# One attention and mixture-of-experts kernel: the work ahead of the first loop in a new order, on other engines and banks

## The chip, the cores and the metric

The kernel runs on one core of one Trainium2 chip. A core has five engines that run side by side, each through its own list of instructions: TensorE (PE; its weight loads are listed apart as PEld), VectorE (DVE), ScalarE (ACT), GpSimd (POOL) and SyncE (SP), which here only issues DMA transfers. They wait for each other through semaphores. Sixteen DMA engines move data between memory and the on-chip buffer; TensorE writes its results into eight banks of a second buffer, PSUM, which VectorE and ScalarE read. The metric is the time of one execution on the device, in microseconds (us).

## What is computed

The input is x, 16 sequences of 512 tokens of 128 numbers. First comes attention with a gated linear recurrence, then a mixture of eight experts with the two best for each token; both are wrapped in layer norms and residuals.

```python
x = x + layernorm(attention(layernorm(x)))
x = x + layernorm(experts(layernorm(x)))

# attention: 16 query heads over 4 key/value heads of 64
q = relu(split(h @ Wq, 16)); k = relu(split(h @ Wk, 4)); v = split(h @ Wv, 4)
g = log_sigmoid(split(h @ Wg1 @ Wg2 + bg2, 4)) / 16
S_t = exp(g_t)[:, None] * S_{t-1} + k_t (outer) v_t ; o_t = (q_t * scale) @ S_t
o = g_norm_weight * o * rsqrt(mean(o**2) + eps)
out = o.reshape(b, t, 1024) @ Wo
```

## The kernel before

The program is in float32. It goes over the 16 sequences one after the other, one turn of a loop for each; a sequence has four tiles of 128 tokens (`NT`) and eight chunks of 64 (`NC`). Within a turn, `chunks(i)` computes the outputs of sequence i chunk by chunk, and between these the next sequence's norm, gates, keys, values, queries and states are prepared: `norm_stats`, `norm_apply`, `norm_transposes`, `gate_logits`, `gates`, `gate_logs`, `gate_sum`, `gate_scan`, `gate_relative`, `decays`, `project_keys`, `project_values`, `key_transposes`, `project_queries_and_states`. The key transposes end in `kJ`, the values in `vJ`, and the state updates (L550) read both; L560 (`scores`) is the first matmul of `chunks`. After the sixteen turns the tokens are sorted to experts, the expert tiles run in a second loop, and a last stage sums and normalises.

Each engine's order is written out by hand. The preparation of sequence 0 has nothing to lie beside, so the same functions run once ahead of the loop, and that stretch is what the change touches. There:

- SP first gives twelve credits to semaphores, then issues the load of the first tokens (`xa`, L380), the eleven loads of the list `WEIGHTS` (L382, with `cst` last, a table of constants of 692 KB that also holds the 0/1 row `in_chunk` for the scan), and the three large expert weights (L384). All count into one semaphore, `weights_in`.
- DVE waits for all of `WEIGHTS`, then makes eight constants (L1262 to L1270, among them the zeroing of `zeros` and `kT`), and only then the statistics of the first tokens (L1026, L1030).
- ACT waits for the weights, for `vJ` to be zeroed and for all eight constants before its table load (L927) and the root of the variance (L767, L769).
- POOL zeroes `vJ` (L1480), applies the norm (L1389), adds the two parts of the gates (`gate_sum`, L1398) and makes them relative to the middle of each chunk (`gate_relative`, L1408). DVE does the scan between these two (L1034).
- PE puts both gate logits (L494, for the head pairs p = 0 and 1) into the one bank `pJ[0]`; the second waits until ACT has read the first twice (L784, L787). Keys, values, key transposes, then all queries mixed with the states follow.

In the loop the functions keep POOL for the norm and for the two gate steps.

## Time and profile before

| | us |
|---|---|
| median of 3 runs | 1332.94 |
| lowest, highest | 1332.85, 1337.09 |
| the profiled execution | 1333.82 |
| its span in the trace | 1332.0 |

PE is busy for 1240.2 us of the span (93%), DVE for 789.2, ACT for 674.4 and POOL for 552.0. The page's chain that ended last lies to 65% on PE. Of 40 equal slices PE is at nine tenths or more in nearly all; the first slice has three tenths, and a few late ones (at the change to the experts and in the last stage) have less.

Times in a trace count from the start of the span. A row gives a start, a duration and what the engine did; `x4` behind it means that four instructions were merged. `[4.09 <-POOL xn L1389]` says that the engine had been idle for 4.09 us and that the named work released it. A float32 matmul leaves two records.

### The profile page before, as it was taken

Reading aid. Unit: us, or ns where it says so; the run is one execution under the profiler, and the core shown is the slowest. Engines: PE = TensorE matmul, PEld = TensorE weight load, DVE = VectorE, ACT = ScalarE, POOL = GpSimd, SP = SyncE. Lnnn points to the kernel's source line nnn. Section 1 sums busy time; section 2 is a strip of 40 time slices with the busy share of each in tenths; the row PEclk is TensorE's granted clock in tenths of the full one; section 3 lists DMA queues with packets and bytes.
Section 4 is the critical chain, followed back from the end, with each engine's and each line's share of the span. In section 5 each row is a group of like instructions: output and inputs, shape, how many; then the busy total and the mean of one; then the engine's idle time right before and its main releaser. Section 6 shows DMA issues by size and latency. Waiting matters only on the chain.

```text
span 1332.0 us, 27589 instructions
## 1 busy us (share of the span) xinstructions
PE 1240.2 (93%) x8008; PEld 1037.8 (78%) x8008; DVE 789.2 (59%) x2374; ACT 674.4 (51%) x1717; POOL 552.0 (41%) x674
## 2 busy tenths in 40 slices
PE   3999999999999999999999999939999999999975
PEld 1778788787787787887877877828899999988952
DVE  2667767767777777677677777643333333333327
ACT  2466565475465665654754656423444444443426
POOL 2223534535436446355354364142333333333326
PEclk9999999999999999999999999969999999999998
DMA  7000100101101001001011010033311111111164
GB/s 274 9 17 9 41 14 26 32 13 34 32 8 40 21 18 40 12 28 32 12 36 32 8 32 16 21 141 106 104 48 48 51 49 48 49 46 44 48 229 178
DMA packets 60282, 67.99 MB, mean 51 GB/s; under 512 B 7488, under 2 KB 50144, under 8 KB 59872
## 3 DMA queue, kind: packets, MB, share of 16 engines
q1 hardware_dynamic: 50656, 46.03, 10.8%
q0 software_dynamic: 8448, 17.45, 4.0%
q10 hardware_dynamic: 1152, 4.19, 1.1%
q8 instruction: 12, 0.20, 0.1%
q14 instruction: 14, 0.11, 0.0%
HBM read 38.50 MB, written 29.15 MB: 51 GB/s over the span
## 4 chain that ended last, share of the span: by engine, by line
PE 65%; DVE 13%; issue 8%; DMA 4%; ACT 4%; POOL 3%; DVEq 1%; SPq 0%; POOLq 0%; ACTq 0%
PE pO L723 8%; PE pA L560 8%; PE pO L576 8%; PE pO L578 6%; PE pW L605 4%; PE pA L714 4%; PE pA L715 4%; PE pJ L714 4%; PE pJ L715 4%; PE pT L588 3%; PE pJ L494 2%; PE pJ L605 2%; DVE S_raw L1076 2%; PE pA L542 2%; DMA expert_out<-y,tail 2%
## 5 line engine op out<-in xcount | busy, mean ns | idle before, releaser
L1524 POOL DMA_INDIRECT expert_out<-y,tail x136 | 130.1, 957 | 264.1 <-ACT y L985 236.9
L576 PE MATMUL pO<-vJ,aT 128*128 128x128 f32 x1024 | 194.1, 279 | 0.0
L578 PE MATMUL pO<-S_mid,qT 128*128 128x128 f32 x896 | 173.2, 275 | 0.0
L840 ACT ACTIVATE sq<-pO 128x512 f32<-128x512 f32 x128 | 75.8, 592 | 184.8 <-PE pO L576 142.2
L576 PEld LDWEIGHTS pO<-vJ,aT 128*128 128x128 f32 x1024 | 153.8, 192 | 14.6 <-issue 13.2
L1099 DVE TENSOR_REDUCE ss<-sq 128x8 f32<-128x512 f32 x128 | 86.5, 676 | 100.6 <-ACT sq L840 100.6
L1458 POOL DMA_INDIRECT expert_rows<-x1n,rowi x120 | 117.1, 976 | 64.9 <-issue 39.5
L578 PEld LDWEIGHTS pO<-S_mid,qT 128*128 128x128 f32 x896 | 136.1, 192 | 0.0
L560 PE MATMUL pA<-qT,kT 128*128 128x256 f32 x512 | 133.3, 383 | 2.5 <-DVE qT L1060 2.5
L723 PE MATMUL pO<-wdown_sb,vJ 128*128 128x128 f32 x1088 | 132.7, 275 | 0.0
L723 PEld LDWEIGHTS pO<-wdown_sb,vJ 128*128 128x128 f32 x1088 | 126.8, 192 | 0.0
L1333 DVE TENSOR_TENSOR vJ<-pA,kJ 128x256 f32<-128x256 f32 x136 | 57.6, 425 | 109.1 <-ACT kJ L976 109.1
L550 PEld LDWEIGHTS pO<-vJ,kJ 128*128 128x128 f32 x448 | 65.2, 190 | 61.8 <-issue 23.1
L605 PE MATMUL pW<-wo_sb,oT 128*128 128x128 f32 x768 | 96.9, 280 | 6.4 <-ACT oT L853 6.4
L1106 DVE TENSOR_TENSOR arena<-pO,rs 128x512 f32<-128x512 f32 x128 | 88.6, 692 | 20.9 <-ACT rs L848 18.9
L605 PEld LDWEIGHTS pW<-wo_sb,oT 128*128 128x128 f32 x768 | 92.4, 195 | 10.2 <-issue 8.3
L560 PEld LDWEIGHTS pA<-qT,kT 128*128 128x128 f32 x512 | 87.4, 191 | 15.5 <-DVE qT L1060 8.9
L853 ACT ACTIVATE oT<-pT,gn_sb 128x512 f32<-128x512 f32 x128 | 86.5, 676 | 22.8 <-PE pT L588 20.7
L985 ACT ACTIVATE y<-pO,tail 128x128 f32<-128x128 f32 x136 | 42.4, 363 | 108.5 <-PE pO L723 88.1
L1333 DVE TENSOR_TENSOR vJ<-pJ,kJ 128x256 f32<-128x256 f32 x136 | 57.6, 425 | 59.0 <-ACT kJ L976 59.0
L1092 DVE TENSOR_TENSOR aT<-pA,cst 128x512 f32<-128x512 f32 x128 | 87.7, 685 | 7.2 <-PE pA L560 7.2
L1425 POOL TENSOR_TENSOR S_mid<-S_raw,step 128x256 f32<-128x256 f32 x112 | 68.4, 617 | 51.6 <-DVE S_raw L1076 34.5
(225 smaller groups left out, 2604.0 us busy)
## 6 DMA issues: line engine op xcount, KB each, us to landing
xt<-expert_rows SPq DMA_DIRECT2D x69, 130.0 KB, 2.2
xa<-x SPq DMA_DIRECT2D x16, 256.0 KB, 2.8
xr<-x SPq DMA_DIRECT2D x16, 256.0 KB, 2.8
after_attention<-x SPq DMA_DIRECT2D x16, 256.0 KB, 2.4
arena<-after_attention ACTq DMA_DIRECT2D x8, 512.0 KB, 3.6
expert_rows<-zeros SPq DMA_DIRECT2D x8, 390.0 KB, 3.1
expert_out<-y,tail POOLq DMA_INDIRECT x136, 2.2
wgate_sb<-wgate SPq DMA_DIRECT2D x1, 2048.0 KB, 9.3
```

The costliest lines, as they stand in the source:

```text
L560: last = mm(pA[c % 2][:, p, :], kT[:, p, c, :], qT[:, p, c, :, :].rearrange("p r c -> p (r c)"), start=True, stop=True)
L576: last = mm(o, aT[:, c % 2, p, h * P:(h + 1) * P], vJ[:, c, p, :], start=True, stop=(c == 0))
L578: last = mm(o, qT[:, p, c, 2 * h:2 * h + 2, :].rearrange("p r c -> p (r c)"), S_mid[:, c, p, :], start=False, stop=True)
L605: last = mm(merge_bank[t], oT[:, t % 2, b, :, :].rearrange("p a c -> p (a c)"), wo_sb[:, b, :], start=(b == 0), stop=(b == PAIRS * R - 1))
L714: mm(bank[f][:, 0:ROWS], wgate_sb[:, e, f * P:(f + 1) * P], xtT[:], start=True, stop=True)
L715: mm(bank[f][:, ROWS:2 * ROWS], wup_sb[:, e, f * P:(f + 1) * P], xtT[:], start=True, stop=True).then_inc(up_psum, 1)
L723: last = mm(ybank[k], hT[:, f, k * P:(k + 1) * P], wdown_sb[:, e, f, :], start=(f == 0), stop=(f == FB - 1))
L1092: v.tensor_tensor(aT[:, c % 2, :, :].rearrange("p a (r c) -> p (a r) c", c=C), pA[c % 2][:].rearrange("p a (r c) -> p (a r) c", c=C), wide ...
L1106: v.tensor_tensor(on[:, c % 2, :, :].rearrange("p k (h d) -> p (k h) d", d=D), pO[c % 2][:].rearrange("p k (h d) -> p (k h) d", d=D), wide ...
L1333: v.tensor_tensor(hT[:, f, :], bank[f][:, ROWS:2 * ROWS], sil[:, f, :], ALU.mult)\
L1458: g.indirect_dma_start(out=xs_dram, in_=x1n[:, k, t, :], in_offset=None, out_offset=bass.IndirectOffsetOnAxis(ap=rowi[:, k, t:t + 1], axis ...
L1524: g.indirect_dma_start(out=ys_dram, in_=y[:, k, :], in_offset=None, out_offset=bass.IndirectOffsetOnAxis(ap=tail[:, k, 1:2].bitcast(U32), ...
```

## The change

The edit leaves the loop, the experts and the last stage as they are, and rewrites the start:

- The small weights (`bg2`, `gnorm`, the router's `rw` and `rb`) become columns of `cst`; the row of 1024 scan constants leaves it, so that it shrinks from 1384 to 379 columns. `wg1` and `wg2` travel as one tile. `in_chunk` is made on POOL.
- ACT issues `cst` and `wg` on its own queue, then loads its table, then waits. SP issues `xa`, `wk`, `wv`, `wq`, `wo`, then gives the twelve credits, then issues the large weights. There are four semaphores (`first_in`, `kv_in`, `q_in`, `rest_in`) in the place of one.
- `kT` and `zeros` are zeroed on POOL. DVE does the statistics first and makes its constants later.
- For sequence 0 the norm, `gate_sum` and `gate_relative` are done by DVE. The gate logits go to `pO[0]` and `pO[1]`.
- ACT copies the first half of the values between the two pairs' decays.
- PE projects the first query ahead of the key transposes, and has four groups of matmuls on a blank bfloat16 tile (20, 4, 6 and 24), whose results nobody reads.

```diff
+            def keep_busy(count, bank):
+                for n in range(count):
+                    mm(bank[:, 0:256], blank[:, 0:P], blank[:], start=True, stop=True)
...
+            for dst, src in FIRST_W:
+                act.dma_start(dst[:], src).then_inc(first_in, 16)
             act.preload_act_table_set(LOG_EXP)
+            act.wait_ge(first_in, 16 * len(FIRST_W))
             norm_rstd(0)
             norm_T(0)
...
-            for p in range(PAIRS):
-                decays(0, p)
+            act.wait_ge(vJ_zero, 1)
+            decays(0, 0)
+            values(0, range(0, 1))
+            decays(0, 1)
             steps_of(0)
-            values(0)
+            values(0, range(1, 2))
             keys(0)
...
             for p in range(PAIRS):
+                dve.wait_ge(lz_ready, p + 1)
+                dve.wait_ge(relz_ready, p + 1)
+                v.tensor_tensor(relz[:, p, :], relz[:, p, :], absz[:, p, :], ALU.add).then_inc(gate_ready, 1)
                 gate_scan(0, p)
+                dve.wait_ge(run_ready, p + 1)
+                r3 = run[:, p, :].rearrange("p (n c) -> p n c", c=C)
+                v.tensor_tensor(rel[:, p, :].rearrange("p (n c) -> p n c", c=C), r3,
+                                wide(r3[:, :, mid:mid + 1], P, NC, C), ALU.subtract).then_inc(rel_ready, 1)
             gate_steps(0)
...
+            g.memset(blank[:], 0.0).then_inc(blank_made, 1)
+            g.memset(in_chunk[:], 1.0).then_inc(scan_made, 1)
+            pool.wait_ge(scan_made, 1)
+            settle(pool)
+            g.memset(in_chunk[:].rearrange("p (n c) -> p n c", c=C)[:, :, 0:1], 0.0).then_inc(scan_made, 1)
+            g.memset(kT[:], 0.0).then_inc(kT_zero, 1)
             g.memset(vJ[:], 0.0).then_inc(vJ_zero, 1)
-            norm_apply(0)
-            for p in range(PAIRS):
-                gate_sum(0, p)
-            for p in range(PAIRS):
-                gate_relative(0, p)
+            g.memset(zeros[:], 0.0).then_inc(zeros_made, 1)
             mids(0)
```

On PE, from its first matmul to the key transposes, stood before (`pJ0` to `pO1` are PSUM banks, `xnT` the normed tokens transposed):

```order
L485 MATMUL pT<-wg2_sb,wg1_sb 128x256 [waits const_made,weights_in]
L481 MATMUL pW<-cst,xn 128x128 [waits xn_ready]
L481 MATMUL pW<-cst,xn 128x128 x3
L494 MATMUL pJ0<-xnT,w12_sb 128x512 [waits xnT_ready,w12_ready]
L494 MATMUL pJ0<-xnT,w12_sb 128x512 [waits relz_ready]
L506 MATMUL pJ0<-xnT,wk_sb 128x512 [waits relz_ready]
L506 MATMUL pJ1<-xnT,wk_sb 128x512
L513 MATMUL pA0<-wv_sb,xnT 128x256 x2
L513 MATMUL pA1<-wv_sb,xnT 128x256 x2
L524 MATMUL pO0<-cst,kT 128x128 [waits k_ready]
```

and stands now, in the same stretch (L680 is the blank matmul):

```order
L680 MATMUL pJ1<-blank 128x256 [waits blank_made]
L680 MATMUL pJ1<-blank 128x256 x19
L504 MATMUL pT<-wg_sb 128x256 [waits first_in]
L680 MATMUL pJ1<-blank 128x256 x4
L500 MATMUL pW<-cst,xn 128x128 [waits xn_ready]
L500 MATMUL pW<-cst,xn 128x128 x3
L680 MATMUL pJ1<-blank 128x256 x6
L513 MATMUL pO0<-xnT,w12_sb 128x512 [waits xnT_ready,w12_ready]
L513 MATMUL pO1<-xnT,w12_sb 128x512
L526 MATMUL pJ0<-xnT,wk_sb 128x512 [waits kv_in]
```

The two waits on `relz_ready` are gone, and thirty blank matmuls stand ahead of the logits. Behind the value projections come the 24 others and one query.

On DVE, from the zeroing of `kT` to the step logs, stood before:

```order
L1267 MEMSET kT 128x2048
L1268 TENSOR_SCALAR nbg2_sb<-bg2_sb 128x2
L1270 CAST zeros<-cst 128x6 [waits const_made]
L1026 BN_STATS st<-xa 128x6 [waits xa_in]
L1026 BN_STATS st<-xa 128x6 x3
L1030 BN_AGGR mv<-st 128x2 [waits xn_stat]
L1030 BN_AGGR mv<-st 128x2 x3
L1273 COPY w12_sb<-pT 128x256 [waits w12_psum]
L1034 SCALAR_TENSOR_TENSOR arena<-cst,arena 128x512 [waits gate_ready] x2
L1042 TENSOR_TENSOR step_log<-arena 128x2x7 [waits rel_ready]
```

and now stands, from the last of its constants to the step logs (L1319 is the sum, L1072 the scan, L1323 the relative step):

```order
L1313 CAST zeros<-cst 128x6 [waits zeros_made]
L1319 TENSOR_TENSOR arena<-arena 128x512 [waits relz_ready,lz_ready,scan_made]
L1072 SCALAR_TENSOR_TENSOR arena<-in_chunk,arena 128x512 [waits gate_ready]
L1323 TENSOR_TENSOR arena<-arena 128x512 [waits run_ready]
L1319 TENSOR_TENSOR arena<-arena 128x512 [waits relz_ready,lz_ready]
L1072 SCALAR_TENSOR_TENSOR arena<-in_chunk,arena 128x512 [waits gate_ready]
L1323 TENSOR_TENSOR arena<-arena 128x512 [waits run_ready]
L1080 TENSOR_TENSOR step_log<-arena 128x2x7 [waits rel_ready]
```

The sum, the scan and the relative step of pair 0 now all stand ahead of the sum of pair 1 on one engine, where two scans stood between four instructions of POOL.

## Rows read from the trace of the kernel before

**Rows 1.** Busy us of each engine by stretch; PEclk, DMA share and GB/s end the row.

```profile
0.00:20.00 20.00, 1.19 (x2) 0.50 (x2) 4.70 (x17) 1.78 (x3) 4.52 (x9) 1.00 0.87 324
29.00:33.00 4.00, 3.61 (x5) 1.54 (x6) 1.81 (x2) 1.48 (x3) 2.21 (x2) 1.00 0.00 0
50.00:80.00 30.00, 29.67 (x221) 26.95 (x221) 20.34 (x41) 19.01 (x46) 9.41 (x11) 1.00 0.04 10
```

**Rows 2.** Timeline of all engines, 0 to 52 us: start, us, engine, work.

```profile
0.73 1.80 POOL L1480 MEMSET vJ<- 128x2048 f32 x1 [0.29 <-POOLq L1604]
1.45 0.44 SPq L380 DMA_DIRECT2D xa<-x  x1
...
11.59 0.23 DVE L1262 CAST tri<-cst 128x128 bf16<-128x128 f32 x1 [11.59 <-DMA cst<-consts]
...
15.14 0.86 DVE L1026 BATCH_NORM_STATS2 st<-xa 128x6 f32<-128x128 f32 x4
...
16.15 0.38 DVE L1030 BATCH_NORM_AGGREGATE mv<-st 128x2 f32<-128x6 f32 x4
...
16.96 0.20 ACT L769 ACTIVATE rstd<-lnv 128x4 f32<-128x4 f32 x1
17.47 3.14 POOL L1389 TENSOR_SCALAR xn<-xa,mv,rstd 128x128 f32<-128x128 f32 x4 [14.94 <-ACT rstd L769]
...
20.67 1.12 PE L481 MATMUL pW<-cst,xn 128*128 128x128 f32 x4 [4.09 <-POOL xn L1389]
...
22.56 2.04 PE L494 MATMUL pJ<-xnT,w_sb 128*128 128x512 f32 x2 [0.78 <-ACT xnT L773]
24.64 0.69 ACT L784 ACTIVATE arena<-pJ,bg_sb 128x512 f32<-128x512 f32 x1 [2.23 <-PE pJ L494]
...
28.07 0.69 ACT L784 ACTIVATE arena<-pJ,bg_sb 128x512 f32<-128x512 f32 x1 [0.98 <-PE pJ L494]
...
29.39 3.78 PE L506 MATMUL pJ<-xnT,wk_sb 128*128 128x512 f32 x4 [1.35 <-ACT arena L787]
29.88 0.63 ACT L800 ACTIVATE arena<-arena 128x512 f32<-128x512 f32 x1
...
32.08 2.06 DVE L1034 TENSOR_TENSOR_SCAN arena<-cst,arena 128x512 f32<-128x512 f32 x1 [2.19 <-POOL arena L1398]
...
35.41 0.18 DVE L1042 TENSOR_TENSOR step_log<-arena 128x14 f32<-128x14 f32 x1 [1.27 <-POOL arena L1408]
35.51 2.84 DVE L1051 SCALAR_TENSOR_TENSOR kT<-pJ,arena 64x512 f32<-64x512 f32 x4
...
36.57 3.17 ACT L827 ACTIVATE vJ<-pA 64x256 f32<-64x256 f32 x8
...
39.22 1.88 PE L542 MATMUL pA<-xnT,wq_sb 128*128 128x512 f32 x4
...
39.77 1.08 ACT L835 ACTIVATE kJ<-pO 128x512 f32<-128x512 f32 x2
...
41.67 0.71 PE L550 MATMUL pO<-vJ,kJ 128*128 128x128 f32 x4 [0.57 <-ACT kJ L835]
...
50.05 2.14 PE L560 MATMUL pA<-qT,kT 128*128 128x256 f32 x8
```

**Rows 3.** DMA issues, 0 to 75 us: KB, then us from issue to landing.

```profile
rw_sb<-rw SPq DMA_DIRECT2D x1, 4.0 KB, 3.2
```

**Rows 4.** DMA issues in the first 1.6 us.

```profile
xa<-x SPq DMA_DIRECT2D x1, 256.0 KB, 2.9
```

**Rows 5.** Timeline of PE within the loop: both records of a gate logit.

```profile
60.58 1.02 PE L494 MATMUL pJ<-xnT,w_sb 128*128 128x512 f32 x2
```

**Rows 6.** DVE lines over the span, shortest, median and longest instruction in ns.

```profile
L1190 DVE TENSOR_SCALAR arena<-x,mv,rstd x4: 335/344/365, 869.5 to 880.8; 128x128 f32<-128x128 f32 x4
...
L1034 DVE TENSOR_TENSOR_SCAN arena<-cst,arena x32: 1214/1215/2060, 28.7 to 809.8; 128x512 f32<-128x512 f32 x32
...
L1375 DVE TENSOR_TENSOR S_mid<-S_mid,arena x2: 679/951/1223, 1327.0 to 1328.1; 128x512 f32<-128x512 f32 x2
```

More of the change, by code:

```diff
@@ L57, with build @@
 ACT_TILES = 6
-C_END = C_PAD + PAD_ROWS
-def build(nc, x, wq, wk, wv, wo, wg1, wg2, bg2, gnorm, rw, rb, wgate, wup, wdown, consts, out):
+C_BG = C_PAD + PAD_ROWS
+C_GN = C_BG + PAIRS
+C_RW = C_GN + 1
+C_RB = C_RW + E
+C_END = C_RB + E
+def build(nc, x, wq, wk, wv, wo, wg, wgate, wup, wdown, consts, out):
     S, L, _ = x.shape
@@ L105, in build @@
         iota8 = cst[:, C_IOTA:C_IOTA + E]
+        bg2_sb = cst[:, C_BG:C_BG + PAIRS]
+        gn_sb = cst[:, C_GN:C_GN + 1]
+        rw_sb = cst[:, C_RW:C_RW + E]
+        rb_sb = cst[:, C_RB:C_RB + E]
         ones_row = cst[:, C_ONES:C_ONES + E]
-        in_chunk = cst[:, C_SCAN:C_SCAN + 1024]
+        in_chunk = sb("in_chunk", [P, L])
         tri = sb("tri", [P, P], BF16)
@@ L246, in build @@
         vJ_zero = sem("vJ_zero")
-        weights_in = sem("weights_in")
+        first_in = sem("first_in")
+        kv_in = sem("kv_in")
+        q_in = sem("q_in")
+        rest_in = sem("rest_in")
+        nbg2_made = sem("nbg2_made")
+        scan_made = sem("scan_made")
+        blank_made = sem("blank_made")
+        kT_zero = sem("kT_zero")
+        zeros_made = sem("zeros_made")
         const_made = sem("const_made")
@@ L817, in steps_of, with values @@
                   scale=-1.0 / GATE_NORMALIZER).then_inc(step_ready, 1)
-            def values(j):
-                for g in range(NT // 2):
+            def values(j, groups=range(NT // 2)):
+                for g in groups:
                     act.wait_ge(v_psum, j * 2 + g + 1)
@@ L1259, in places @@
                 v.tensor_copy(rows_at[:, :, part], rowf[:, :, part]).then_inc(rowi_ready, 1)
-            dve.wait_ge(weights_in, 16 * len(WEIGHTS))
+            norm_stats(0)
+            dve.wait_ge(first_in, 16 * len(FIRST_W))
+            v.tensor_scalar(nbg2_sb[:], bg2_sb, -1.0, None, ALU.mult).then_inc(nbg2_made, 1)
+            dve.wait_ge(xn_rstd, 1)
+            for t in range(NT):
+                v.tensor_scalar(xn[:, t, :], xa[:, t, :], mv[:, 0, t, 0:1], rstd[:, 0, t:t + 1],
+                                ALU.subtract, ALU.mult).then_inc(xn_ready, 1)
+            dve.wait_ge(w12_psum, 1)
+            v.tensor_copy(w12_sb[:].rearrange("k p j -> k (p j)"), pT[:, 0:PAIRS * P]).then_inc(w12_ready, 1)
             v.tensor_copy(tri[:], cst[:, C_TRI:C_TRI + P]).then_inc(const_made, 1)
```

96 lines of the change are left out of this document (51 added, 45 removed).

## The prediction

> **What bounds the kernel now.** I read the busy time by stretch first. In the first 20 us PE works for 1.19 us, while in the loop (50 to 80 us) it works for 29.67 of 30 [rows 1]. So the loop is bound by PE and the change leaves it alone; what can be won lies ahead of 50.05, where the first `scores` start [rows 2]. From there every engine's work hangs on that matmul in the same order as before, so a start that comes earlier by some us should bring the end forward by as much.
>
> The timeline of that stretch is a relay with one runner at a time [rows 2]. DVE is released by `cst` at 11.59. It makes constants until 15.14, does the statistics until 16.53 (16.15 + 0.38), and ACT's root ends at 17.16. POOL applies the norm until PE transposes at 20.67. PE starts the first logit at 22.56 and ACT reads it at 24.64. ACT's second pair starts at 28.07 after 0.98 us of waiting for PE and ends at 30.51. Sum, scan and relative step of pair 1 lead to the step logs at 35.41; `kT` is done at 38.35; the copies into `kJ` start at 39.77 behind ACT's value copies and let PE go on at 41.67. From 41.67 to 50.05 PE alternates states and queries, the same before and after the edit.
>
> **The sum, leg by leg.** Each leg is the time before less the time after.
>
> 1. *Loads and statistics.* Three things leave the path: twelve credits ahead of `xa`, ten loads and the large `cst`, and DVE's constants. `xa` was issued at 1.45 [rows 2] behind the credits; POOL's own first work starts at 0.73 [rows 2], so I take 0.8. It landed 2.9 us after its issue [rows 4], which gives 3.7. The statistics took 1.39 (15.14 to 16.53) and end at 5.1 instead of 16.53: **11.4**. If SP cannot issue before 1.45, this is 0.65 less. ACT also needs `cst` and `wg`, two issues of some 0.44 each [rows 2] from 0.75 on; a small load landed in 3.2 [rows 3], so `wg` is in at 4.4, ahead of the statistics. The table load lies in this wait too. The load of the next tokens is issued some 13 us earlier, still behind the large weights. By 29 no DMA runs any more [rows 1], and the next tokens are not read before the chunks begin, at 31 by this sum.
> 2. *The root* keeps its 0.63 and ends at 5.75.
> 3. *The norm.* On POOL it took 3.51 (17.16 to 20.67) [rows 2]. Four like instructions on DVE took 335 to 365 ns each [rows 6]: 1.4, with the hand-over 1.45. Gain **2.05**; xn is ready at 7.2.
> 4. *Transposes.* Both records of a gate logit took 2.04 at 22.56 [rows 2] and take 1.02 in the loop [rows 5]. PE therefore runs at half its later pace at the start, 1.2 GHz against 2.4. The four transposes (1.12) would take 0.56: gain **0.55** if the blank matmuls have brought PE to full pace by 7.2. The first logit then starts at 8.5.
> 5. *First logit.* 2.08 (22.56 to 24.64) becomes 1.08: gain **1.0**. ACT begins at 9.6.
> 6. *Second bank.* The second logit no longer waits for ACT, so the 0.98 of idle time [rows 2] goes. Both pairs take 4.9 instead of 5.87 (24.64 to 30.51): **1.0**. ACT ends at 14.5, with pair 0 done at 12.05.
> 7. *Sum, scan, relative.* DVE has six instructions in a row. A scan takes 1.215; a 128x512 sum of two on-chip tiles took 0.679 undisturbed [rows 6]. That is 2 x (0.68 + 1.215 + 0.68) = 5.15, with six hand-overs of some 0.05 it is 5.45, so 12.1 + 5.45 = 17.55. From ACT's end this is 3.05 where it was 4.9 (30.51 to 35.41): **1.85**. Pair 1's sum is queued behind pair 0's relative step for 0.3 us; this is counted. Bound above: the disturbed prices 1.223 and 2.06 [rows 6] would make the six 9.0, 3.9 us later. I take the undisturbed ones since POOL, once its memsets are over, has nothing to do until the states.
> 8. *Keys.* Step logs to the end of `kT` keep 2.94 (35.41 to 38.35) and end at 20.5.
> 9. *Values and `kJ`.* Eight value copies took 3.2 (36.57 to 39.77) [rows 2] and held the `kJ` copies back. Now four of them fit between pair 0's decays (over at 16.0) and pair 1's at 17.6. Pair 1's two decays and the step take some 1.15 (35.41 to 36.57), the other four values 1.6: ACT is free at 20.35, while the first group of key transposes ends at some 20.9. With 1.9 for the copies (39.77 to 41.67), PE goes on at 22.8, 2.3 behind `kT` instead of 3.3: **0.95**.
>
> Sum: 11.4 + 2.05 + 0.55 + 1.0 + 1.0 + 1.85 + 0.95 = **18.8 us**.
>
> What is costed at nothing: the 24 blank matmuls behind the values. 256 columns at 2.4 GHz are 0.107 us, so 2.6 in all. PE starts the logits at 8.5; two logits, two keys (0.86 each, half of the 1.88 of L542 less its overlap [rows 2]) and the values end near 13.6, the blanks at 16.2, and the first query must wait for values at 17.6 anyway. The cover is 1.4 us. The query itself (0.9) ends at 18.5; pair 0's transposes wait for `kT` at 19.1. POOL's memsets: 2048 columns take 1.80 [rows 2], so blank, `in_chunk`, `kT`, `vJ` and `zeros` together (some 5,400 columns) are done at about 5.8. `vJ` is wanted at 14.8, `kT` at 17.6. SP's credits now stand behind five issues; the loop needs them at 31. DVE's constants (about 1 us) fall behind `w12` at 7.6 and are over before 12.1.
>
> **Two rules weighed.** The column PEclk shows 1.00 from 29 to 33 us [rows 1], where four records of 512 columns took 3.78 against 1.88 for a like four at 39.22 [rows 2]. I go by the durations and count the column as having no record yet. The Trainium skill, "TensorE: Matmul & The Clock Gate", Part 1, warns that the clock gate's trace events have been seen to be unreliable; by the column alone, legs 4 and 5 would be nothing, and the sum 17.25.
>
> The second scan took 2.06 while POOL's L1408 ran beside it, the median of 32 is 1.215 [rows 2, 6]. The Trainium skill, "GPSIMD Engine Reference", section 8, says that GpSimd shares its interfaces to the on-chip buffer with VectorE and contends with instructions that read two tiles there. It speaks against giving POOL 5 us of memsets, if these reach into leg 3; the norm at the same factor of 1.7 would cost 1.0 more and the sum would be 17.8. No row shows a memset beside DVE.
>
> **Rivals.**
>
> *A. The blank matmuls do not lift PE in time, or stand in its way.* Twenty at 1.2 GHz are 4.3 us (0.213 each), so they end at 5.2; then the small product and four more end at about 7.2, just as xn arrives. For it: this leaves no slack, and a blank one could cost more than its columns; a float32 record of 512 columns took 0.94 at half pace (3.78 / 4), which would bound one of 256 at 0.47, and make twenty 9.4. PE came to full pace somewhere between 29.39 and 39.22, that is in less than 9.8 us of nearly steady work. Against it: the blanks begin at 0.95 and PE then has 7 us of steady work before the logits. If the clock rises only around 10, legs 4 and 5 fall out (1.55), six blanks reach 0.5 past the copy, and the twenty delay the start by some more: a gain of 15 to 17, **1317**. If it does not rise at all before the states, logits, keys, values, 24 blanks and the query take 4.1 + 3.8 + 3.8 + 5.1 + 1.9 from 9.6, PE goes on near 31, and the gain is 10.6: **1322**.
>
> *B. The first loads land later.* `cst` and `wg` go on a second queue over the same DMA engines, beside `xa`, keys, values and queries. Each us past 5.1 costs one. At 6.5: a gain of 17.4, **1315.5**. At worst they come behind the large weights, at about 24: nothing is left, **1333**, no change.
>
> *C. Slower.* The early blank work leaves PE at half pace into the loop. There each us of PE's work then costs a second one, as it is busy 99% [rows 1]; it decides at 19 us of such work (38 us of time). The whole of 52 us at half pace would give away 26: **1340**. Against it: with the same loop behind it PE was at full pace from 39.22 on, and nothing in the edit takes work away there.
>
> **How the numbers follow.** The profiled execution took 1333.82, 0.88 above the median of 1332.94. Its own time less 18.8 is 1315.0; from the median it is **1314.1**, my number. Chances: the forecast within 1.5 us 0.62; up to 2.5 us better (loads in 2.4, cheaper norm) 0.06; A in part 0.18, A in full 0.03; B by a us or two 0.07, B in full 0.02; C 0.02. Legs 1, 3 and 7 carry bounds of 0.65, 1.0 and 3.9. The range 1311.5 to 1319 holds the forecast, the better case, A in part and B by little, and leaves out about 1 in 10. Faster by over 0.3% (about what a measurement of this kernel tells from no change) 0.96, within it 0.02, slower 0.02.
>
> **What would show it.** Statistics ending at 5.1 (leg 1); xn to PE in 1.5 (3); both records of the first logit in 1.02 (4, 5); no idle ACT between the pairs (6); step logs at 17.5 (7); L570, the states, at 22.8 (9); the first L580 at 31.2; and a loop of unchanged length. I am wrong if the blanks end after xn is ready, if ACT waits for `first_in` past 5.1, or if the time from the first scores to the end is not 1282 us as it is now (1332.0 - 50.05).

## The result, and the profile after

| | before | after |
|---|---|---|
| median, us (4 runs each, on one chip) | 1333.66 | 1319.48 |
| lowest, highest | 1332.85, 1337.09 | 1318.53, 1321.94 |
| the profiled execution | 1333.82 | 1320.18 |
| its span | 1332.0 | 1318.4 |
| first `scores` | 50.05 | 32.96 |
| from there to the end of the span | 1281.95 | 1285.44 |

The ratio is 0.9892, with a 95% interval of 0.9869 to 0.9915. The change makes the kernel 1.1% faster, on the side that was forecast, but 5.4 us short of 1314.1 and a little past the upper end of 1319.0. The last two rows say where the shortfall lies. The start gained 17.1 us and not 18.8. Then 3.5 us were lost behind it, in code that the change doesn't touch.

The timeline of the new start (start, us, engine, work) answers to [rows 2]:

```profile
0.73 0.44 SPq L393 DMA_DIRECT2D xa<-x  x1
0.74 0.45 ACTq L959 DMA_DIRECT2D cst<-consts  x1
...
1.09 4.24 PE L680 MATMUL pJ<-blank 128*128 128x256 bf16 x20 [1.09 <-POOL blank L1531]
...
4.50 0.87 DVE L1064 BATCH_NORM_STATS2 st<-xa 128x6 f32<-128x128 f32 x4 [4.50 <-DMA xa<-x]
...
6.57 1.12 DVE L1304 TENSOR_SCALAR xn<-xa,mv,rstd 128x128 f32<-128x128 f32 x4 [0.62 <-ACT rstd L803]
...
7.74 0.66 PE L500 MATMUL pW<-cst,xn 128*128 128x128 f32 x4 [1.24 <-DVE xn L1304]
...
9.34 3.11 PE L513 MATMUL pO<-xnT,w_sb 128*128 128x512 f32 x4
...
11.35 0.69 ACT L818 ACTIVATE arena<-pO,cst 128x512 f32<-128x512 f32 x1 [2.33 <-PE pO L513]
...
13.71 0.67 ACT L818 ACTIVATE arena<-pO,cst 128x512 f32<-128x512 f32 x1
...
19.19 0.18 DVE L1080 TENSOR_TENSOR step_log<-arena 128x14 f32<-128x14 f32 x1
...
22.68 1.09 ACT L869 ACTIVATE kJ<-pO 128x512 f32<-128x512 f32 x2 [0.50 <-PE pO L544]
...
24.58 0.71 PE L570 MATMUL pO<-vJ,kJ 128*128 128x128 f32 x4 [0.54 <-ACT kJ L869]
...
32.96 2.14 PE L580 MATMUL pA<-qT,kT 128*128 128x256 f32 x8
```

Of each leg it tells the following.

| leg | forecast | measured |
|---|---|---|
| 1, statistics end | 5.1 | 5.90 |
| 3, norm to PE | 1.45 | 1.21 (6.53 to 7.74) |
| 4 and 5, transposes to ACT's first read | 2.4 | 3.61 (7.74 to 11.35) |
| 6, ACT over both pairs | 4.9 | 4.78, and no idle time at 13.71 |
| 7, ACT's end to step logs | 3.05 | 3.06 (16.13 to 19.19) |
| 8 and 9, step logs to states | 5.25 | 5.39 (19.19 to 24.58) |
| first `scores` | 31.2 | 32.96 |

So two legs missed, 1 by 0.8 us and 4 with 5 by 1.2. The others agree to 0.25. In a second profile of the same kernel (after_again, below) the first `scores` come at 33.19.

Busy us of each engine by stretch (PE, PEld, DVE, ACT, POOL), with PEclk, DMA share and GB/s at the end of a row, answer to [rows 1] and show the second miss:

```profile
6.50:7.70 1.20, 0.00 (x0) 0.00 (x0) 1.14 (x5) 0.03 (x1) 0.00 (x0) 1.00 1.22 475
7.70:8.20 0.50, 0.47 (x4) 0.47 (x5) 0.50 (x3) 0.00 (x0) 0.00 (x0) 1.00 1.12 451
8.20:9.30 1.10, 1.10 (x8) 0.83 (x7) 0.25 (x4) 0.60 (x1) 0.00 (x0) 0.59 0.90 369
9.30:10.00 0.70, 0.70 (x3) 0.38 (x2) 0.00 (x0) 0.00 (x0) 0.00 (x0) 0.50 1.00 421
...
11.90:13.00 1.10, 1.10 (x4) 0.53 (x3) 0.00 (x0) 1.10 (x3) 0.00 (x0) 1.00 0.85 358
```

The blanks had done their work: the transposes took 0.66, not 1.12. But PE stood idle from 6.50 to 7.74, since four blanks do not reach to xn. The granted clock fell from 2.4 to 1.2 GHz near 8.4, though PE was at work again, and rose near 11.8. The first logit lies in the slow part.

The loss behind the start is the harder one. I took the shift between the two profiles (time before less time after, at the same instruction): 17.1 at the first `scores`, 17.3 in turns 4 to 16, and 17.2 at the first transposes of an expert tile (897.00 against 879.77). So the loop, and the sorting behind it, kept the gain. At the last tile it is 14.5 (1278.19 against 1263.72), at the end 13.6. Counted from 0, most of the 69 tiles take 5.46 us in both; the first, tiles 2, 4, 6 and 8 and tile 58 are longer in both. In after, tiles 10, 35 and 59 take 6.92, 6.68 and 7.16. In before these three are normal (5.46, 5.46, 5.53) and tile 52 takes 6.87. Three sound tiles turned long and one long tile turned sound. They are long for two different reasons.

Row transposes of tiles 35 and 36 on PE, after:

```profile
1078.32 0.38 PE L732 MATMUL pT<-cst,xt 128*128 128x128 f32 x2
...
1085.00 0.44 PE L732 MATMUL pT<-cst,xt 128*128 128x128 f32 x2 [1.06 <-DMA xt<-expert_rows]
```

and before:

```profile
1094.12 0.38 PE L698 MATMUL pT<-cst,xt 128*128 128x128 f32 x2
...
1099.58 0.38 PE L698 MATMUL pT<-cst,xt 128*128 128x128 f32 x2
```

The waits of after between 1078 and 1085.5 (us in total, times, longest) lead back from there:

```profile
POOL expert_out L1577 <- ACT y L1023: 4.9, 1, 4.9
ACT y L1023 <- DVE tail L1389: 3.1, 1, 3.1
DVE tail L1389 <- POOLq L1582: 2.7, 1, 2.7
...
PE pT L732 <- DMA xt<-expert_rows: 1.1, 1, 1.1
```

PE waits for the rows `xt`, whose load waited for VectorE, which waited for POOL's queue, which waits at L1582 for the scatter of output rows to land. The DMA queues over the two scatters of this tile (after, 1076.5 to 1080; packets, MB, share) show a guest:

```profile
q8 instruction: 1, 0.02, 2.2%
...
expert_out<-y,tail POOLq DMA_INDIRECT x2, 3.1
```

The 3.1 behind `x2` is the median of the two. Taken alone, the first scatter (1076.61) landed in 2.2 and the second (1077.87), with the packet at 1079.57 beside it, in 4.0. The same tile before (1092.3 to 1096) has no such packet, and its scatters land in 2.2:

```profile
q0 software_dynamic: 64, 0.13, 11.0%
...
expert_out<-y,tail POOLq DMA_INDIRECT x2, 2.2
```

The page's list of queues has, for the whole execution of after (packets, MB, share):

```profile
q8 instruction: 12, 0.20, 0.1%
```

So there are twelve such packets of 16 KB, and their name says that they carry an engine's own instructions. Which engine's, the runs below tell. At tile 10 of after, the scatter in flight beside such a packet took 4.2, and at tile 52 of before 3.8.

The last of the twelve, at 1273.47, meets the very last scatter of after, and the load of the last stage waits for that one. It landed in 6.2 (1272 to 1278); in before the last scatter has no packet beside it and landed in 4.8 (1286.5 to 1292):

```profile
expert_out<-y,tail POOLq DMA_INDIRECT x1, 6.2
```

```profile
expert_out<-y,tail POOLq DMA_INDIRECT x1, 4.8
```

Tile 59 is another matter. No packet stands there. In every profile of this case, before's too, PE waits about 2 us for the rows `xt` at the end of tile 58. PE in after:

```profile
1212.87 0.44 PE L732 MATMUL pT<-cst,xt 128*128 128x128 f32 x2 [2.02 <-DMA xt<-expert_rows]
1213.15 3.49 PE L757 MATMUL pO<-wdown_sb,vJ 128*128 128x128 f32 x16
```

```profile
1214.00:1216.50 2.50, 2.50 (x14) 2.50 (x13) 0.34 (x2) 0.00 (x0) 0.00 (x0) 0.50 0.08 26
```

and in one_queue, a run below whose tile 59 is sound:

```profile
1209.81 0.44 PE L734 MATMUL pT<-cst,xt 128*128 128x128 f32 x2 [2.11 <-DMA xt<-expert_rows]
1210.09 1.96 PE L759 MATMUL pO<-wdown_sb,vJ 128*128 128x128 f32 x16
```

Behind the pause the granted clock fell to 1.2 GHz for some 3 us in after (0.50 in the stretch from 1214.0 to 1216.5), and the sixteen records took 3.49 and not 1.96. This is the loss of legs 4 and 5 once more. It fell so in the ten profiles whose tile 59 is long, and stayed at 1.00 in before, before_longer, aligned and one_queue, with pauses of 1.95 to 2.13 us in all fourteen. Why the same pause lets it fall in some and not in others isn't shown, nor whether it goes by the kernel or by the execution: only after has a second profile, and there it fell too.

### The profile page after: what moved, and what is told of

It is laid out like the page before. It is cut to its first block, busy times and chain, and to the rows that moved or that the text cites. A ratio compares the mean times of both kernels' runs of the same rounds, so it can differ in the third digit from the quotient of the medians.

```text
span 1318.4 us, 27696 instructions
## 1 busy us (share of the span) xinstructions
PE 1243.6 (94%) x8062; PEld 1043.3 (79%) x8062; DVE 789.3 (60%) x2380; ACT 675.0 (51%) x1717; POOL 547.5 (42%) x671
## 4 chain that ended last, share of the span: by engine, by line
PE 66%; DVE 13%; issue 8%; DMA 5%; ACT 4%; POOL 3%; DVEq 1%; POOLq 0%; SPq 0%; ACTq 0%
PE pO L757 8%; PE pA L580 8%; PE pO L596 8%; PE pO L598 6%; PE pW L625 4%; PE pA L748 4%; PE pA L749 4%; PE pJ L748 4%; PE pJ L749 3%; PE pT L608 3%; DMA expert_out<-y,tail 2%; DVE kT L1089 2%; DVE S_raw L1114 2%; PE pJ L625 2%; PE pA L562 2%
## 5 line engine op out<-in xcount | busy, mean ns | idle before, releaser
L887 ACT ACTIVATE oT<-pT,cst 128x512 f32<-128x512 f32 x128 | 86.6, 677 | 22.6 <-PE pT L608 20.8
```

## The experiments

All are edits of after, unless said. "Tiles" is the time from the first to the last row transposes, "long" lists tiles of the four (10, 35, 52, 59) that took over 6.3 us in that kernel's profile. Medians are of four or more runs, and the ratio is against before on the same chip. The kernels were taken on several chips, on which before's own median was 1332.94 (the row here; also for after_again, no_blanks, gap_filled and pool_gates), 1333.53 (late_blanks, aligned, one_queue and one_bank), 1333.66 (after) and 1334.00 (the other four), so over all rows it is the ratios that compare.

| kernel | median | ratio, 95% | first `scores` | tiles | long |
|---|---|---|---|---|---|
| before | 1332.94 | | 50.05 | 381.19 | 52 |
| after | 1319.48 | 0.9892 (0.9869, 0.9915) | 32.96 | 383.95 | 10, 35, 59 |
| after_again | 1319.62 | 0.9889 (0.9873, 0.9905) | 33.19 | 383.28 | 10, 35, 59 |
| no_blanks | 1317.48 | 0.9877 (0.9862, 0.9892) | 33.64 | 381.62 | 52, 59 |
| gap_filled | 1319.09 | 0.9888 (0.9873, 0.9903) | 32.33 | 384.34 | 10, 35, 59 |
| pool_gates | 1325.20 | 0.9934 (0.9920, 0.9947) | 38.43 | 384.36 | 10, 35, 59 |
| late_blanks | 1321.85 | 0.9910 (0.9894, 0.9927) | 33.44 | 383.43 | 10, 35, 59 |
| aligned | 1318.00 | 0.9884 (0.9868, 0.9901) | 31.98 | 380.27 | 52 |
| one_queue | 1317.00 | 0.9878 (0.9862, 0.9895) | 30.92 | 381.36 | 10, 35 |
| one_bank | 1319.64 | 0.9890 (0.9874, 0.9907) | 35.43 | 384.19 | 10, 35, 59 |
| one_queue_aligned | 1316.15 | 0.9866 (0.9851, 0.9882) | 31.39 | 381.63 | 52, 59 |
| before_longer | 1336.76 | 1.0020 (1.0011, 1.0029) | 50.19 | 382.18 | 10, 35 |
| old_query_values | 1320.66 | 0.9898 (0.9882, 0.9913) | 33.09 | 384.21 | 10, 35, 59 |
| one_queue_no_blanks | 1318.52 | 0.9881 (0.9866, 0.9896) | 32.41 | 382.46 | 52, 59 |

**Is the loss a matter of chance?** The changed kernel, unchanged, once more:

> The changed kernel once more, unchanged. In its first profile the first scores start at 32.96 us, 17.1 us earlier than before (50.05), but the end comes only 13.6 us earlier; 3.5 us were lost between the first scores and the end, nearly all in the expert tiles, at tiles whose scatter of output rows finished late (before: one such tile among tiles 10 to 57, at 1187 us; after: two, at 940 and 1078 us, and one more at 1213). Theory 'chance': these late scatters fall where they like in any execution, so this profile has the first scores at 33.0 again (within 0.2) and another number of long tiles, the stretch behind the first scores is 1282 to 1287 us, and over five rounds the gain over the kernel before is near 17 us (15 to 18). Theory 'systematic': the new start brings the later stages into a worse position; the same tiles are long again and the gain stays at 13 to 14.5 us.

The same three tiles are long. The theory that a scatter meets something at random falls; what hits tiles 10 and 35 belongs to the program. The clock at the start does vary: here PE's pause ahead of the transposes was 1.56 us, and the clock had fallen before they began (1.11, not 0.66).

**What are the blanks worth?** All four groups taken out:

```diff
-            keep_busy(20, pJ[1])
...
-            keep_busy(4, pJ[1])
...
-            keep_busy(6, pJ[1])
...
-            keep_busy(24, pW)
```

> The changed kernel without its 54 blank matmuls. In the changed kernel PE's granted clock is full from about 5.2 us, falls to half at about 8.4 (after PE had idled from 6.50 to 7.74) and rises at 11.9, so the first logit (9.34) ran at half pace although the blanks were there. Theory 'the blanks miss': without them the transposes take 1.1 instead of 0.7 and the logit starts at about 9.6, ScalarE's first read begins at 11.7 to 11.9 (11.35 with them), the step logs at 19.5 to 19.8 (19.19), the first scores at 33.2 to 33.8 (32.96): less than 1 us slower. Rival 'the blanks carry the start': keys, values and states run at half pace too and the first scores come at 35 or later, 2 us or more slower.

The logit is then slow from end to end (timeline of no_blanks):

```profile
7.69 1.11 PE L500 MATMUL pW<-cst,xn 128*128 128x128 f32 x4 [1.50 <-DVE xn L1300]
...
9.59 3.75 PE L513 MATMUL pO<-xnT,w_sb 128*128 128x512 f32 x4 [0.78 <-ACT xnT L803]
```

and the first `scores` come 0.45 to 0.7 later than in after and its repeat. Yet the median is 2.1 lower than that of after_again. The intervals of the two ratios overlap, so this is likely and not proven; in the profiles the tiles take 1.7 less, as 10 and 35 are sound again and 52 is long, as in before. If so, the blanks cost more in the experts than they bring at the start, and not by what they do there: they had ended at 18.5. The one thing of them that lasts is that PE's list of instructions is longer, by 54 weight loads and 54 matmuls.

**Does the idle 1.24 us let the clock fall?** The four blanks become fifteen:

```diff
-            keep_busy(4, pJ[1])
+            keep_busy(15, pJ[1])
             norm_transposes(0)
```

> The changed kernel with 15 blank matmuls in the place of 4 ahead of the transposes, which at 0.107 us each reach over the 1.24 us in which PE idled (6.50 to 7.74). Theory 'the idle time dropped the clock': the granted clock stays at full from about 5.2 on, six blanks take 0.65, the first logit starts at 9.1 and takes 1.02, ScalarE's first read begins at 10.2 instead of 11.35, the step logs at 18.1 (19.19) and the first scores at 31.8 (32.96): 1.0 to 1.3 us faster than the changed kernel. Rival 'it falls anyway' (transposes or blanks on zeros don't hold it): the granted clock drops near 8.4 again, the first read begins at 11.3 to 11.6 and nothing is gained, or up to 0.5 us is lost as the blanks stand before the transposes.

```profile
6.50 1.81 PE L680 MATMUL pJ<-blank 128*128 128x256 bf16 x15
...
9.53 1.95 PE L513 MATMUL pO<-xnT,w_sb 128*128 128x512 f32 x4
10.72 0.69 ACT L818 ACTIVATE arena<-pO,cst 128x512 f32<-128x512 f32 x1 [1.34 <-PE pO L513]
```

The logits take 1.95 and not 3.11, and from the transposes to ACT's read it is 2.57 in place of 3.61: 1.0 of the missing 1.2. The granted clock is 1.00 throughout. Some 0.3 of it goes again, as the fifteen run past xn (ready near 7.9, transposed at 8.15), and `xa` landed 0.14 later, so the first `scores` come 0.6 to 0.9 earlier and not the 1.0 to 1.3 expected. The median moved by only 0.5, within the spread, and the tiles stayed as long; in this kernel tile 63 takes 6.87 as well, and there too a packet of queue 8 (between 1234 and 1236) stands beside a scatter, which takes 4.2. With 22 instructions more than after, the packet that met after's last scatter at 1273.47 comes here, and the last scatter lands in 5.3.

**Norm and gate steps back on POOL** (legs 3 and 7):

```diff
-            for t in range(NT):
-                v.tensor_scalar(xn[:, t, :], xa[:, t, :], mv[:, 0, t, 0:1], rstd[:, 0, t:t + 1],
-                                ALU.subtract, ALU.mult).then_inc(xn_ready, 1)
...
+            norm_apply(0)
+            for p in range(PAIRS):
+                gate_sum(0, p)
+            for p in range(PAIRS):
+                gate_relative(0, p)
             mids(0)
```

> The changed kernel with the norm, the sums and the relative steps of sequence 0 back on GpSimd; all else stays. Theory of the forecast: the norm costs 3.5 instead of 1.4 us up to the transposes, and from the end of ScalarE's gates to the step logs it takes 4.9 again instead of 3.1, with the second scan at 2.06 beside GpSimd: 3.5 to 4.2 us slower than the changed kernel, first scores at 36.5 to 37.2. Rival: PE idles longer, the clock stays at half longer, and another 0.5 to 1 us comes on top. If the gates on VectorE were worth nothing, the first scores would stay at 33.

```profile
20.67 2.06 DVE L1072 TENSOR_TENSOR_SCAN arena<-in_chunk,arena 128x512 f32<-128x512 f32 x1 [1.09 <-POOL arena L1438]
...
24.00 0.18 DVE L1080 TENSOR_TENSOR step_log<-arena 128x14 f32<-128x14 f32 x1 [1.27 <-POOL arena L1448]
```

The transposes begin at 10.05, 2.3 later than in after, and the step logs 4.8 later. The scan beside POOL's L1448 takes 2.06 again, as in [rows 2], where after has 1.23. The first `scores` are 5.5 later and the median 5.6 higher. This is more than the 3.5 to 4.2 of the theory: 0.6 more goes at the transposes and the first logit, which stay at half pace throughout, as the rival said, and 0.7 between the step logs and `kJ`. This is the largest single part after the loads.

**Is it the length of PE's code?** No blanks at the start, but 54 of them in the pause ahead of the expert tiles, where PE waits anyway. The start is then that of no_blanks and the code behind as long as after's:

```diff
             pe.wait_ge(tail_in, 16 * len(BIG))
+            pe.wait_ge(an_ready, S * NT)
+            keep_busy(54, pW)
             pe.wait_ge(counts_ready, 1)
```

> No blank matmuls at the start, but 54 of them in the 11 us in which PE idles between the last ranks and the first expert tile (868.5 to 879.8 in the changed kernel). The kernels with 54 or 65 blanks at the start have their long tiles at 10 and 35 in every profile, the one without any has one at 52, as the kernel before; each of these tiles has a 16 KB instruction packet beside its scatter of output rows. Theory 'code length': what counts is how much of PE's code lies ahead of the tile loop, so the long tiles are at 10 and 35 again although the start has no blanks; first tile about 1.3 us shorter (5.5 instead of 6.2 to 7.7) as PE's clock is up when it begins; first scores at 33.6 as without blanks. Rival 'early work': the blanks at the start disturb by what they do there (clock or timing); then the long tile stays at 52.

Tiles 10 and 35 are long again (6.51 and 6.73), as in after, and 52 is sound. The last scatter lands in 6.2, where it took 5.4 in no_blanks. The median is 4.4 above no_blanks, and the intervals of the ratios don't overlap. In the profiles 0.7 of it lies ahead of the first tile, 1.8 in the tiles and 1.3 behind them. That the late blanks would shorten the first tile did not come true: it took 6.58, and 6.21 without them.

In the next kernel the blanks at the start are 20, 11, 4 and 24, and 69 follow late, 128 in all. That makes 256 instructions more than without blanks. The Trainium skill, "Trainium Architecture — The Big Picture", "The software stack", gives an instruction 64 bytes, so by estimate a 16 KB packet holds 256 of them. The runs show the 16 KB and, here, the return of the pattern with 256 instructions more.

```diff
-            keep_busy(4, pJ[1])
+            keep_busy(11, pJ[1])
             norm_transposes(0)
-            keep_busy(6, pJ[1])
+            keep_busy(4, pJ[1])
...
+            pe.wait_ge(an_ready, S * NT)
+            keep_busy(69, pW)
             pe.wait_ge(counts_ready, 1)
```

> The changed kernel with 11 blanks instead of 4 ahead of the transposes and 4 instead of 6 behind them (59 in all), and 69 more in PE's idle stretch ahead of the expert tiles: 128 blanks are 256 instructions or one 16 KB packet of code more than none. Theory 'code length': the packets come at the same tiles as without blanks, so the long tile is at 52 and none at 10 and 35; the clock is held at the start, first scores at 31.9 to 32.4; first tile 5.5; the stretch behind the first scores takes 1281 to 1283; the time is 1314 to 1316, faster than any so far. Rival 'more work ahead costs anyway': 10 and 35 are long and the stretch behind the first scores stays at 1284.5 to 1286, the time at 1318 to 1319.

Tiles 10 and 35 are sound, 52 is long (7.15), and the tiles take 3.7 us less than in after. Not all of that is the packets': tiles 10, 35 and 52 together give 1.0, tile 59, where the clock held, 1.6, and the first five 1.1. The last scatter lands in 5.5, in place of 6.2. A packet falls on the scatters of tile 52 (1168 to 1174; the median of 2.2 and 4.1):

```profile
q8 instruction: 1, 0.02, 1.5%
...
expert_out<-y,tail POOLq DMA_INDIRECT x2, 3.2
```

With more instructions than after, and not fewer, the pattern is that of before. So it is not that there are more of them, but where the packets fall. The start has the clock at 1.00 all through, and ACT reads the first logit at 10.37, 2.63 behind the transposes. What the 69 late ones gave back is 1.7 us ahead of the first tile, for which they were too many. The median of 1318.00 misses the 1314 to 1316 that was expected, and by its ratio this kernel can't be told from after.

The strongest case is the kernel before itself with 54 tiny matmuls in the same pause, and nothing else:

```diff
             pe.wait_ge(tail_in, 16 * len(BIG))
+            pe.wait_ge(an_ready, S * NT)
+            for n in range(54):
+                mm(pW[:, 0:E], ones[:], ones[:, 0:E], start=True, stop=True)
             pe.wait_ge(counts_ready, 1)
```

> The kernel before, with nothing changed but 54 matmuls of eight columns in PE's idle stretch between the last ranks and the first expert tile (885.5 to 897.0). It does the start as before, so its first scores are at 50.05. Theory 'code length': PE's code ahead of the tile loop is as long as in the changed kernel, so its long tiles are at 10 and 35 and not at 52, its tile stretch takes 383 to 384.3 instead of 381.2, and it is 1 to 2.5 us slower than the kernel before. Rival 'the changed start does it': the long tile stays at 52 and the time is that of the kernel before.

It is slower, 1.0020 (1.0011 to 1.0029), by 2.8 us of the medians. Its first tile starts at 897.08, where before's does at 897.00, so the tiny matmuls themselves cost nothing. Tile 52 is sound and 10 and 35 are long (6.76 and 6.48). Nothing was added but instructions of PE, so queue 8 carries PE's code. Tile 35's scatters of before_longer (1093 to 1099), to be held against the same tile in after and before above (3.0 is the median of 2.2 and 3.9):

```profile
q8 instruction: 1, 0.02, 1.1%
...
expert_out<-y,tail POOLq DMA_INDIRECT x2, 3.0
```

In its profile the tiles are 1.0 longer (1.3 and 1.0 at tiles 10 and 35, 1.4 back at 52), the last scatter lands in 6.3 in place of 4.8, and the whole span is 1.6 longer. The 383 to 384.3 expected of the tiles was too much (382.18), as it counted tile 59 in, which is sound here. The rest of the 2.8 isn't located by a trace. The profiled run was the shortest of its eleven (1335.41) and had the highest mean granted clock, 0.984; eight of the others had 0.981 or 0.982, where only two of before's fifteen beside them had less than 0.983. So the clock, at tile 59 or elsewhere, is a likely part of it.

**Why did the first tokens land late?** `cst` and `wg` go on SP behind `xa`, and ACT issues nothing:

```diff
             sp.dma_start(xa[:], seq(xv, 0)).then_inc(xa_in, 16)
+            for dst, src in FIRST_W:
+                sp.dma_start(dst[:], src).then_inc(first_in, 16)
...
-            for dst, src in FIRST_W:
-                act.dma_start(dst[:], src).then_inc(first_in, 16)
```

> The changed kernel with the constants and wg issued by SyncE behind xa, in the place of ScalarE's own queue. The statistics started at 4.50 (xa issued at 0.73, 3.8 us to land), where the forecast had 3.7 (2.9 to land, as the kernel before showed). Theory 'the second queue shares the DMA engines with xa': xa alone in front lands in 2.9 to 3.1 again, the statistics start at 3.7 to 3.9, and wg, issued at 1.7, lands at 5.0 to 5.4, so ScalarE's root waits for it or not by a little; net first scores 0.3 to 0.8 earlier than 33.0. Rival 'the first transfer of an execution is slow to start, whatever is beside it': the statistics start at 4.5 again and the first scores come at 33 or up to 0.5 later.

```profile
3.46 0.87 DVE L1064 BATCH_NORM_STATS2 st<-xa 128x6 f32<-128x128 f32 x4 [3.46 <-DMA xa<-x]
...
4.95 0.30 ACT L803 ACTIVATE lnv<-mv,cst 128x4 f32<-128x4 f32 x1 [2.93 <-DVE mv L1068]
...
8.12 1.96 PE L515 MATMUL pO<-xnT,w_sb 128*128 128x512 f32 x4
```

The statistics start 1.04 earlier. In all nine profiles of the kernels with two queues `xa` took 3.7 to 3.9, in all three of those with one queue 2.7 to 2.9. Whether it is the second queue or only that `cst` is issued 0.5 sooner, these runs don't separate. PE's pause ahead of the transposes is 0.41 and the clock stays at 2.4 GHz, so the first `scores` come at 30.92, 2.0 earlier where 0.3 to 0.8 was expected. This is the 31.2 of the forecast and a little better. Tiles 10 and 35 are long as in after, which has the same code length on PE; 59 is sound. The ratio of 0.9878 is below after's two, with intervals that overlap.

**The second bank** (leg 6). Both logits in `pJ[0]` again, with the two waits:

```diff
-            return pO[p][:].rearrange("p k v -> p (k v)") if at_start(j) else pJ[0][:]
+            return pJ[0][:]
...
-                if not at_start(j):
-                    pe.wait_ge(relz_ready, j * 2 + 2)
+                pe.wait_ge(relz_ready, j * 2 + 2)
```

> The changed kernel with both gate logits of sequence 0 in bank pJ0, as before: the second waits until ScalarE has read the first twice. Forecast's leg 6: 1.0 us at half pace (0.98 of waiting in the kernel before). PE idles while it waits, so the clock stays at half: the first scores come 1.0 to 1.5 later than 33.0. Rival: VectorE is the bound behind the gates (its six instructions of sum, scan and step in a row end 1.0 after ScalarE would let them), so pair 1's logs are wanted only when pair 0's relative step is over, and one bank costs 0.5 or less.

```profile
14.01 0.69 ACT L817 ACTIVATE arena<-pJ,cst 128x512 f32<-128x512 f32 x1
...
19.36 0.18 DVE L1079 TENSOR_TENSOR step_log<-arena 128x14 f32<-128x14 f32 x1
...
22.10 1.41 DVE L1088 SCALAR_TENSOR_TENSOR kT<-pJ,arena 64x512 f32<-64x512 f32 x2 [1.22 <-ACT arena L842]
...
25.15 1.08 ACT L868 ACTIVATE kJ<-pO 128x512 f32<-128x512 f32 x2 [0.85 <-PE pO L543]
```

ACT's second pair starts at 14.01, only 0.3 later than in after, of which 0.17 stood at its first pair already. And the step logs are not later for it: 7.84 behind ACT's first read in both kernels (11.52 to 19.36; 11.35 to 19.19), as VectorE's six steps set that time. The bank pays in another place. Here the keys wait for ACT's second reads (to 15.41), at half pace, and the values follow at 18.75, where after has them at 14.01. ACT's first value copies, which stand between the pairs' decays, so hold pair 1's decays back until 21.43, and `kT` waits for these. `kJ` comes 2.2 later than in the repeat of after, and the `scores` 2.2 to 2.5. The four runs lie far apart (two at 1317.7, two above 1321), so the median doesn't show it; the timeline does.

**The query ahead, the values split** (leg 9), both undone:

```diff
-            project_queries_and_states(0, range(0, 1))
             key_transposes(0, range(NC // 2))
-            project_queries_and_states(0, range(1, 2 * PAIRS * R))
+            project_queries_and_states(0)
...
             decays(0, 0)
-            values(0, range(0, 1))
             decays(0, 1)
             steps_of(0)
-            values(0, range(1, 2))
+            values(0)
```

> The changed kernel with the first query behind the key transposes and all value copies behind both pairs' decays, as before. Leg 9 of the forecast: ScalarE is at the copies of kJ about 1 us later, so the states and the first scores come 0.8 to 1.2 later than 33.0. Rival: the key transposes are the bound there, nothing is lost (0.3 at most).

```profile
18.26 0.18 DVE L1078 TENSOR_TENSOR step_log<-arena 128x14 f32<-128x14 f32 x1
...
19.42 3.18 ACT L860 ACTIVATE vJ<-pA 64x256 f32<-64x256 f32 x8
...
22.62 1.08 ACT L868 ACTIVATE kJ<-pO 128x512 f32<-128x512 f32 x2
```

In this profile the clock stayed up at the logits and the step logs came at 18.26. Its start up to there is that of after; only the first twenty blanks took 4.45 where they took 4.24, so that the four behind them reached to 7.04 and the pause was 0.74 instead of 1.24. I compare from the step logs on: to `kJ` 4.36 against 3.49, to the first `scores` 14.83 against 13.77. The leg is worth 1.0 at the `scores`; 0.95 was forecast.

**Is there a better version?** One queue, with 74 tiny matmuls in the late pause to make it 128:

```diff
+            for dst, src in FIRST_W:
+                sp.dma_start(dst[:], src).then_inc(first_in, 16)
...
+            pe.wait_ge(an_ready, S * NT)
+            for n in range(74):
+                mm(pW[:, 0:E], ones[:], ones[:, 0:E], start=True, stop=True)
             pe.wait_ge(counts_ready, 1)
...
-            for dst, src in FIRST_W:
-                act.dma_start(dst[:], src).then_inc(first_in, 16)
```

> The version with one queue for the first loads (first scores at 30.92, long tiles at 10, 35 and 58) with 74 matmuls of eight columns added in PE's idle stretch ahead of the expert tiles, so that 128 blank matmuls in all make PE's code one 16 KB packet longer than without any. Theory 'code length': the long tiles at 10 and 35 go and one comes at 52; the tile stretch from first to last takes 380.3 to 381.5 as in the other kernel of that length; since they are small they don't push the first tile back (the 69 large ones did by 1.7): first scores at 30.9, span 1312 to 1313.5, time 1314 to 1315.5. Rival 'the long tiles are no loss on the whole' (what is gained at one tile is waited for at another): the span stays at 1314 or more.

It has the lowest median and the lowest ratio of all, 0.9866; by the ratios it is about 3 us below after and after_again, with intervals that just overlap theirs. The 1314 to 1315.5 expected was missed. Tiles 10 and 35 are sound, 52 is long and the last scatter lands in 5.2 (6.3 in one_queue), but the clock fell at tile 59. That takes back what was hoped for against one_queue, from which its ratio can't be told. Here ACT's root waited for `wg`, the third load of the one queue, which costs 0.5:

```profile
5.42 0.30 ACT L806 ACTIVATE lnv<-mv,cst 128x4 f32<-128x4 f32 x1 [3.40 <-DMA wg_sb<-wg]
```

Last, one queue and no blanks, whose edit is the sum of the two shown:

> One queue for the first loads and no blank matmul anywhere. PE's code ahead of the tile loop is as long as in the kernel before, so there is one long tile at 52 beside 58. The clock: PE's first work is the small product at about 5, transposes at 6.7, logits at 8.4, all at half pace: ScalarE's first read begins at 10.6 to 10.8 (9.32 with blanks), the first scores come at 32.3 to 32.8 (30.92). Time 1315.5 to 1317, 1 to 2 us slower than the version with one queue and 128 blanks. Rival: blanks are worth nothing even with the clock held (first scores at 31.2 or earlier).

Its first `scores` come at 32.41, 1.0 to 1.5 later than in the two kernels with one queue and blanks. So where the clock holds, the blanks are worth what rival A's arithmetic said (legs 4 and 5, 1.55), and half of that in after, where it fell. In the median this doesn't show: its ratio of 0.9881 can't be told from theirs, 0.9878 and 0.9866, and 1318.52 misses the expected 1315.5 to 1317.

## Why the prediction was right or wrong

**Leg 1 was 0.8 too large.** The step that failed is "It landed 2.9 us after its issue [rows 4]". In before the next load was issued 0.5 us behind `xa`, on the same queue; in after `cst` is issued in the same moment on ACT's queue, and `xa` took 3.7. one_queue, with `cst` behind it again, has 2.7. Rival B named this mechanism and, with 0.07, gave it too little.

**Legs 4 and 5 were 1.2 too large.** The blanks did bring PE to full pace, near 5.3 (the product of the gate weights behind the first twenty took 0.69, and 1.19 in no_blanks), so rival A's "do not lift PE in time" is wrong. The step that failed is the silent one that once up, the clock stays up: I had the blanks end "just as xn arrives", saw only the danger that they end late ("this leaves no slack"), and didn't price a pause behind them. The four ended at 6.50 and not at 7.2, as PE had come to full pace before them, and xn came 0.5 late, by leg 1: a pause of 1.24 us. gap_filled and aligned close the pause and get 2.57 and 2.63 for these legs, against 2.4 forecast. The profiles order themselves by the pause. It was 1.24 (after), 1.32 (one_bank), 1.56 (after_again) and 3.80 us (pool_gates) where the clock fell, and at most 0.74 (old_query_values) where it held. In size this is rival A in part.

**Legs 3, 6, 7, 8 and 9 held**, each within 0.25, and leg 7 took the undisturbed prices: 0.69, 1.23 and 0.69, where pool_gates shows the 2.06 that was the bound. The norm of 1.12 beside no memset leaves the rule that speaks against POOL's memsets without a case: POOL was done at 5.93 and the norm began at 6.57. Leg 6 was right in the length of ACT's stretch but not in what the bank is worth: with one bank the step logs come at the same distance, and 2.2 to 2.5 us are lost at the keys and values, where 1.0 was forecast.

**The loop did as forecast.** Rival C didn't come: in turns 4 to 16 the shift is 17.3. What failed is the step that carried the whole sum to the end: "a start that comes earlier by some us should bring the end forward by as much", and with it the last test, 1282 us from first `scores` to the end, which came to 1285.4. About 2.8 of these 3.5 us lie in the expert tiles (383.95 against 381.19), 0.9 behind the last, and the traces show two causes.

The first is PE's code. Tiles 10 and 35 lose 1.46 and 1.22 and tile 52 gives 1.39 back, 1.3 in sum; the last scatter, 6.2 in place of 4.8, costs 1.4 more, of which the last stage regains some 0.5. This cause is shown by runs in both directions: 108 instructions more on PE move the fetches of its code so that they meet the scatters of tiles 10 and 35 and the last one instead of tile 52. late_blanks and before_longer make the same tiles long without any blank at the start, and aligned restores the old ones with 256 more. The last scatter took 6.0 to 6.3 in the eight profiles with a packet beside it, 4.8 to 5.5 in the other six. A fetch alone does no harm: in before one stands at 1036.48, between the scatters of 1033.61 and 1037.80, and both land in 2.2. It has to meet the landing that POOL waits for.

The second is the clock at tile 59, 1.6 us. It does not go by the code's length: the tile is long in no_blanks and sound in one_queue, the other way about than tiles 10 and 35. It may well go by the execution, as one_queue's profiled run had a mean granted clock of 0.984 and its three others 0.981. The traces show the fall, and no run here was made to steer it, so what decides it stays open. Both causes together are 3.8 us; the first tiles and the stretch ahead of them give 0.3 back.

**Open.** Why the clock falls behind the pause at tile 58 in ten profiles and not in four. And why runs of one kernel spread over 3 us, so that gap_filled's earlier start of 0.6 to 0.9 can't be seen in its median; the clock has a likely part in this, as the runs of a kernel with the higher mean granted clock tend to be the shorter ones (in one_bank 0.982 went with 1317.7 twice, 0.981 and 0.980 with 1321.6 and 1323.6), but nothing isolates it.

By the profiles, the forecast for the profiled run was 1315.0 and it took 1320.18. Of these 5.2 us, 1.8 are legs 1, 4 and 5, and 3.4 are the step to the end.

## What to carry to other kernels

A kernel that is bound by one engine gives the whole gain of a shorter start only if nothing else is moved, and adding instructions, even where they cost nothing, moves the fetches of the code behind them. Compare the shift between two profiles at a dozen places, not at the end alone; where it steps down, look for a packet on the instruction queue, and for a granted clock that fell behind a pause. Work that holds the clock up should reach to the next real work, and the very first load should be issued ahead of all others, on one queue with them.

## What was not expected of the hardware

- A fetch of 16 KB of PE's instructions beside a scatter of rows delayed its landing from 2.2 to between 3.7 and 4.4 us, and lengthened the tile by 0.9 to 1.7. The last scatter of the loop took 6.0 to 6.3 with one beside it and 4.8 to 5.5 without.
- PE's granted clock fell from 2.4 to 1.2 GHz near 8.4 us, behind 1.24 us of idle time that followed some five us of nearly steady matmuls. It didn't fall where the pause was 0.41 (one_queue), 0.46 (aligned) or 0.74 (old_query_values). Behind one of 1.95 to 2.13 at tile 59, after hundreds of us of work, it fell in ten profiles of fourteen.
- Matmuls on a blank tile of zeros, read by nobody, kept the clock at 1.00.
- A load issued on a second queue in the same moment as the first one made that take 3.7 us instead of 2.7.
